# Attention scores and row maxima as pairs of 64-row TensorE tiles, in steps of two PSUM banks

## The reference, cut to what matters

```python
xn = _layernorm(x)
x = x + _L0_attn_ref(xn, Wq, Wk, Wv, Wo) + _L0_ffn_ref(xn, W1, b1, W2, b2)          # full softmax, gelu, 2048 hidden
xn = _layernorm(x)
x = x + _L1_attn_ref(xn, w_qkv, b_qkv, w_dense, b_dense) + _L1_ffn_ref(xn, w12, b12, w3, b3)  # causal, rotary, gate, 512 hidden
# in both attentions: 32 query heads and 8 key heads of 16
scores = jnp.einsum('bhqd,bhkd->bhqk', q, k) * scale
probs = jax.nn.softmax(scores, axis=-1)
out = jnp.einsum('bhqk,bhkd->bhqd', probs, v)
```

## Time and profile before

| | us |
|---|---|
| median of 3 runs | 635.09 (633.90 to 636.69) |
| the profiled execution | 634.52 |
| its span, first to last instruction | 632.8 |
| TensorE matmuls busy in the span | 586.8 (93%) |
| VectorE, ScalarE, GpSimd busy | 438.4, 356.3, 213.8 |
| granted TensorE clock, mean | 0.985 |

### The profile page before, as it was taken

The page is one execution under the profiler, slowest core; times in us unless marked ns, Lnnn a source line. Parts: engine busy times, 40 slices in busy tenths (PEclk is TensorE's granted clock), DMA queues, the critical chain, the costliest instruction groups (busy, mean ns, idle before and its releaser), DMA issues.

```text
span 632.8 us, 10359 instructions
## 1 busy us (share of the span) xinstructions
PE 586.8 (93%) x3360; PEld 452.0 (71%) x3360; DVE 438.4 (69%) x815; ACT 356.3 (56%) x611; POOL 213.8 (34%) x332
## 2 busy tenths in 40 slices
PE   3788899999999999999999999897999999899985
PEld 2677677787777787677877767666777877667754
DVE  6559967656566576486897685867796887487552
ACT  2337766754564683666585564655655564474440
POOL 5703423122303331111322122443643455254231
PEclk9989999999999999999999999999899999999989
DMA  5574541353233334324543323244433353344001
GB/s 187 173 207 151 134 118 67 102 150 101 69 82 103 99 101 118 84 67 134 151 134 100 85 68 117 84 105 114 127 92 102 84 142 110 85 121 116 2 17 51
DMA packets 29805, 67.30 MB, mean 106 GB/s; under 512 B 4788, under 2 KB 17588, under 8 KB 27704
## 3 DMA queue, kind: packets, MB, share of 16 engines
q1 hardware_dynamic: 21112, 38.32, 22.2%
q0 software_dynamic: 8640, 28.32, 15.2%
HBM read 51.67 MB, written 14.68 MB: 105 GB/s over the span
## 4 chain that ended last, share of the span: by engine, by line
PE 74%; ACT 6%; DVE 6%; DMA 5%; issue 5%; POOL 2%; SPq 1%; ACTq 0%; DVEq 0%; POOLq 0%
PE banks L693 48%; PE banks L748 8%; PE banks L800 7%; PE banks L778 7%; PE banks L753 2%; DMA q_sb<-q_parts 2%; DMA raw<-in_attn 1%; PE banks L781 1%; PE banks L713 1%; ACT L917 1%; ACT probs L917 1%; ACT hid_f L937 1%; ACT L936 1%; POOL probs L649 1%; DMA q_sb<-max_t 1%
## 5 line engine op out<-in xcount | busy, mean ns | idle before, releaser
L1067 DVE TENSOR_REDUCE neg_max<-banks 128x2 f32<-128x512 f32 (+1 forms) x256 | 158.1, 620 | 150.4 <-PE banks L748 93.7
L917 ACT ACTIVATE probs<-banks 128x512 f32<-128x512 f32 (+1 forms) x256 | 137.8, 545 | 193.8 <-PE banks L778 145.6
L693 PE MATMUL banks<-xnT,w_up 128*128 128x512 f32 x576 | 157.4, 407 | 5.4 <-issue 3.7
L693 PE MATMUL banks<-w_down,hid 128*128 128x512 f32 x480 | 129.4, 403 | 4.2 <-ACT hid_f L937 2.0
L693 PEld LDWEIGHTS banks<-xnT,w_up 128*128 128x128 f32 x576 | 102.9, 192 | 33.4 <-issue 13.9
L748 PEld LDWEIGHTS banks<-k_sb,q_sb 96*128 96x128 f32 x512 | 93.6, 193 | 22.7 <-issue 5.6
L693 PEld LDWEIGHTS banks<-w_down,hid 128*128 128x128 f32 x480 | 87.0, 191 | 31.8 <-DVE neg_max L1067 6.7
L748 PE MATMUL banks<-k_sb,q_sb 96*128 96x256 f32 (+1 forms) x512 | 100.3, 278 | 4.8 <-DMA q_sb<-q_parts 4.2
L649 POOL TENSOR_SCALAR_AFFINE_SELECT probs<-probs 128x256 f32<-128x256 f32 x128 | 57.6, 450 | 111.5 <-ACT probs L917 106.6
L778 PE MATMUL banks<-q_sb,k_sb 97*128 97x512 f32 x192 | 79.3, 413 | 11.7 <-ACT probs L917 11.1
L693 PE MATMUL banks<-xnT,w_qkv 128*128 128x256 f32 x576 | 83.7, 293 | 2.3 <-DVE xnT L1011 1.4
(11 more groups left out here) (78 smaller groups left out, 629.3 us busy)
## 6 DMA issues: line engine op xcount, KB each, us to landing
q_sb<-q_parts SPq DMA_DIRECT2D x64, 256.0 KB, 4.7
raw<-in_up POOLq DMA_DIRECT2D x48, 256.0 KB, 3.0
raw<-in_down POOLq DMA_DIRECT2D x40, 256.0 KB, 3.0
q_parts<-stage SPq DMA_DIRECT2D x32, 256.0 KB, 2.6
raw<-in_attn POOLq DMA_DIRECT2D x20, 256.0 KB, 3.1
k_parts<-stage SPq DMA_DIRECT2D x16, 256.0 KB, 2.5
k_sb<-k_parts SPq DMA_DIRECT2D x16, 256.0 KB, 4.2
x_res<-in_x SPq DMA_DIRECT2D x4, 512.0 KB, 4.1
```

The costliest lines, as they stand in the source:

```text
L693: mm = nc.tensor.matmul(out_ap, lhs(a), rhs(b_), start=first and j == 0, stop=stop and j == 2, **kw)
L917: nc.scalar.activation(probs[:, i, 0:w], banks[:, ST_BANKS[k % 2], 0:w], ACT.Exp, scale=SCALES[n // B]).then_inc(exp_done, 1)
L1067: nc.vector.tensor_reduce(neg_max[:, s, 2 * g:2 * g + 2, t], banks[:, bank_of[x], :].rearrange("p (r t) -> p r t", r=2)[:, :, 0:w], AX.X, ...
```

## The change

Queries and keys of a head are held as 48 rows (three of 16: the three products of parts), and the maximum is row 48. Half of the heads lie in rows 0 to 48 and the other half in rows 64 to 112, so that a step issues its matmuls in pairs, one in each half of the array's rows, each into a bank of its own. A unit has four steps of `st` and four of `m`, each with four heads and two banks, in slots 0, 2, 4 and 6; an `st` step waits for the exponential of the step before it. `m` has banks 2 and 3 to itself, and three banks are left to the rest. The mask is put in first, by a part of its own ahead of `st`. `pv` stands directly behind `m` in slots 0 and 4, `mt` in slot 4; a down's addition comes behind the next step of TensorE. Keys of two sequences fit. The zeros are gone; the ones come by DMA. GpSimd's clearing is a step of its own (`tri`), one slot behind `st`.

```diff
-ROWS = 96
-MROW = 96
+HALF = 64
+ROWS = 48
+MROW = 48
+SOON = -1
+STEPS = 4
...
 ST_BANKS = (0, 1)
-WORK_BANKS = (2, 3, 4, 5, 7)
+MAX_BANKS = (2, 3)
+WORK_BANKS = (4, 5, 7)
 PV_BANK = 6
 HID = 4
 HT = 4
 
-COST = {"up": 681, "down": 681, "wo": 693, "qkv": 363, "xn": 440, "v": 220, "st": 233, "m": 250, "mt": 110, "pv": 995}
+COST = {"up": 681, "down": 681, "wo": 693, "qkv": 363, "xn": 440, "v": 220, "st": 330, "m": 240, "mt": 110, "pv": 995}
...
+    if x[0] == "m":
+        return 1 if x[1] < LU else 2
     return {"up": 4, "down": 2, "wo": 4, "qkv": 8}.get(x[0], 1)
...
 def cost(x):
+    if x[0] == "part" and x[1][0] == "m":
+        return 300
     return COST.get((x[1] if x[0] == "part" else x)[0], 0)
...
     if x[0] == "down":
-        return [(1, ("add",) + x[1:])]
+        return [(SOON, ("add",) + x[1:])]
     if x[0] == "split":
         return [(1, ("low", x))]
+    if x[0] == "st" and x[1] >= LU:
+        return [(1, ("tri",) + x[1:])]
     return []
...
-    o = []
+    soon, o = [], []
     for g, slot in enumerate(slots):
-        head = [k for k, x in enumerate(slot) if x[0] in ("st", "m")]
+        head = [k for k, x in enumerate(slot) if x[0] in ("st", "m", "pv")]
         cut = head[-1] + 1 if head else 0
         for x in slot[:cut] + due[g] + slot[cut:]:
             o.append(x)
+            if cost(x):
+                o += soon
+                soon = []
             for d, y in followers(x):
                 if d == 0:
                     o.append(y)
+                elif d == SOON:
+                    soon.append(y)
                 else:
                     due[g + d].append(y)
...
-    o += [parts(("qkv", 0, 0)) + [("load_k", 0, 0), ("load_k", 0, 1)]]
+    o += [parts(("qkv", 0, 0)) + [("load_k", 0)]]
-    ms = spread([[("m", 0, i)] for i in range(8)], parts(("qkv", 1, 2)), [1] * 8)
+    ms = spread([[("m", 0, j)] for j in range(STEPS)], parts(("qkv", 1, 2)), [1] * STEPS)
     later = parts(("up", 0, 1, 0)) + parts(("qkv", 1, 0)) + [("bias",)]
-    ms += spread([[("m", 1, i)] for i in range(4)], later, [1] * 4)
-    ms[8] += [("mt", 0), ("mrow", 0)]
-    ms[9] += split(0, "up", 2, 3)
-    ms[10] += split(0, "down", 0, 1)
+    ms += spread([[("m", 1, 0)], [("m", 1, 1)], [], []], later, [1] * 4)
+    ms[4] += [("mt", 0), ("mrow", 0)]
+    ms[5] += split(0, "up", 2, 3)
+    ms[6] += split(0, "down", 0, 1)
...
-    slots = [[("st", u, i)] for i in range(8)]
-    for i in range(8):
-        if i < 4 and u + 1 < UNITS:
-            slots[i].append(("m", u + 1, i + 4))
-        if i >= 4 and u + 2 < UNITS:
-            slots[i].append(("m", u + 2, i - 4))
+    slots = [[] for _ in range(8)]
+    for j in range(STEPS):
+        w, i = (u + 1, j + 2) if j < 2 else (u + 2, j - 2)
+        maxima = parts(("m", w, i)) if w < UNITS else []
+        slots[2 * j] += maxima[:-1] + [("st", u, j)] + maxima[-1:]
+    if u > 0:
+        slots[0].append(("pv", u - 1, 1))
+    slots[4].append(("pv", u, 0))
     if s == 2 and n + 1 < 2 * B:
-        slots[0].append(("load_k", n + 1, 0))
-    if s == 0 and n > 0:
-        slots[0].append(("load_k", n, 1))
+        slots[0].append(("load_k", n + 1))
     if 0 < u < UNITS - 2:
         slots[0].append(("load_q", u + 2))
     if u > 0:
-        slots[1].append(("pv", u - 1, 1))
-        slots[2].append(("norm", u - 1, 0))
-        slots[3] += [("norm", u - 1, 1), ("norm", u - 1, 2)]
-        slots[4].append(("norm", u - 1, 3))
-        slots[5].append(("ctx", u - 1))
+        slots[1].append(("norm", u - 1, 0))
+        slots[2] += [("norm", u - 1, 1), ("norm", u - 1, 2)]
+        slots[3].append(("norm", u - 1, 3))
+        slots[4].append(("ctx", u - 1))
     if u + 1 < UNITS:
-        slots[5] += [("mt", u + 1), ("mrow", u + 1)]
-    slots[5].append(("pv", u, 0))
...
+        if x[0] == "m" and x not in bank:
+            bank[x] = ST_BANKS if x[1] == 0 and x[2] % 2 else MAX_BANKS
+            before[x] = user.get(bank[x])
+            user[bank[x]] = x
+        elif (x in wk or x[0] == "up") and x not in bank:
-        if y:
+        if y and y[0] != "m":
...
-    qscr = nc.dram_tensor("q_parts", (2 * B, S, 2 * HD, UH * T), F32, kind="Internal").ap()
-    kscr = nc.dram_tensor("k_parts", (2 * B, 4, HD, NKV * T), F32, kind="Internal").ap()
+    qscr = nc.dram_tensor("q_parts", (2 * B, S, 2, P, T), F32, kind="Internal").ap()
+    kscr = nc.dram_tensor("k_parts", (2 * B, 2, P, T), F32, kind="Internal").ap()
...
-        q_sb = sb("q_sb", [P, RING, UH, T], F32R)
-        k_sb = sb("k_sb", [P, NKV, T], F32R)
+        q_sb = sb("q_sb", [P, RING, UH // 2, T], F32R)
+        k_sb = sb("k_sb", [P, 2, NKV // 2, T], F32R)
...
+                    sp_.wait_ge(made, ONES)
+                    for row in (MROW, HALF + MROW):
+                        sp_.dma_start(k_sb[row:row + 1, :, :, :].rearrange("o a c t -> o (a c t)").bitcast(F32),
+                                      ones[0:2 * NKV // 2 * T // P, :].bitcast(F32)).then_inc(ones_loaded, 16)
...
-                    if pair < 2:
-                        for j in range(2):
-                            dst = qscr[n, 2 * pair + j].rearrange("(h d) (g t) -> (d g) h t", h=2, g=UH)
-                            sp_.dma_start(dst, stage[:, k % 2, :, j, :].bitcast(F32)).then_inc(staged[k % 2], 16)
-                    else:
-                        for j in range(2):
-                            dst = kscr[n].rearrange("(h e) d (g t) -> e (d g) h t", e=2, g=NKV)[j]
-                            sp_.dma_start(dst, stage[:, k % 2, :, 0, :].bitcast(F32)).then_inc(staged[k % 2], 16)
+                    for j in range(2 if pair < 2 else 1):
+                        dst = qscr[n, 2 * pair + j] if pair < 2 else kscr[n]
+                        sp_.dma_start(dst.rearrange("h q t -> q h t"),
+                                      stage[:, k % 2, :, j, :].bitcast(F32)).then_inc(staged[k % 2], 16)
...
-                    for e in range(2):
-                        sp_.dma_start(q_sb[32 * e:32 * e + 32, u % RING, :, :].rearrange("p g t -> p (g t)").bitcast(F32),
-                                      qscr[n, s]).then_inc(q_loaded[u % RING], 16)
+                        sp_.wait_ge(st_filled, st_index(u - RING, STEPS - 1) + 1)
+                    rows = qscr[n, s].rearrange("h (e a d c) t -> a (h e) d (c t)", e=2, a=2, c=4)
+                    for a in range(2):
+                        to = q_sb[HALF * a:HALF * a + ROWS, u % RING, :, :].rearrange("p c t -> p (c t)").bitcast(F32)
+                        sp_.dma_start(to[0:2 * HD], rows[a]).then_inc(q_loaded[u % RING], 16)
+                        sp_.dma_start(to[2 * HD:], rows[a, 0:2]).then_inc(q_loaded[u % RING], 16)
...
-                    _, n, f = x
-                    k = stg[("store", n, 2)]
-                    sp_.wait_ge(staged[k % 2], 32 * (k // 2 + 1))
-                    if n:
-                        sp_.wait_ge(st_filled, st_index(S * (n - 1) + 2 * f + 1, 7) + 1)
-                    g = slice(4 * f * T, (4 * f + 4) * T)
-                    sp_.dma_start(k_sb[0:4 * HD, 4 * f:4 * f + 4, :].rearrange("p g t -> p (g t)").bitcast(F32),
-                                  kscr[n].rearrange("q d x -> (q d) x")[:, g]).then_inc(k_loaded[f], 16)
+                    n = x[1]
+                    wait_stored(sp_, stg[("store", n, 2)])
+                    if n > 1:
+                        sp_.wait_ge(st_filled, st_index(S * (n - 1) - 1, STEPS - 1) + 1)
+                    rows = kscr[n].rearrange("h (e a d c) t -> a (h e) d (c t)", e=2, a=2, c=4)
+                    for a in range(2):
+                        to = k_sb[HALF * a:HALF * a + ROWS, n % 2, :, :].rearrange("p c t -> p (c t)").bitcast(F32)
+                        sp_.dma_start(to[0:HD], rows[a, 0:2]).then_inc(k_loaded[n % 2], 16)
+                        sp_.dma_start(to[HD:], rows[a]).then_inc(k_loaded[n % 2], 16)
...
-                    sp_.dma_start(q_sb[MROW:MROW + 1, u % RING, :, :].rearrange("o h t -> o (h t)").bitcast(F32),
-                                  max_t[:, u % 2, :].bitcast(F32)).then_inc(m_loaded[u % RING], 16)
+                    for a in range(2):
+                        row = HALF * a + MROW
+                        sp_.dma_start(q_sb[row:row + 1, u % RING, :, :].rearrange("o c t -> o (c t)").bitcast(F32),
+                                      max_t[8 * a:8 * a + 8, u % 2, :].bitcast(F32)).then_inc(m_loaded[u % RING], 16)
...
-            nc.gpsimd.memset(k_sb[64:ROWS, :, :].bitcast(F32), 0.0).then_inc(made, 1)
-            pool.wait_ge(made, 3)
-            load(4)
-            load(5)
-            nc.gpsimd.memset(k_sb[MROW:MROW + 1, :, :].bitcast(F32), 1.0).then_inc(made, 1)
-            pool.wait_ge(made, 4)
-            for k in range(RING):
-                load(6 + k)
-                nc.gpsimd.memset(q_sb[64:ROWS, k, :, :].bitcast(F32), 0.0).then_inc(made, 1)
-                pool.wait_ge(made, 5 + k)
+            for k in range(4, EARLY):
+                load(k)
```

(52 more changed lines are left out.)

102 lines of the change are left out of this document (38 added, 64 removed).

## The result

The changed kernel took 671.88 us in the median of 4 runs (668.45 to 673.13), the kernel before 634.50 (632.97 to 636.69): a ratio of 1.0578, with an interval of 1.0526 to 1.0629. Forecast were 612 us and a gain; what came was 37 us of loss.

The account below looks back on a forecast made before the run. PE's own work was taken to set the time. Terms of -17, -9, -6, -2, +10 and +2 summed to -22 us against 634.5, giving 612.5, called 612, with a range of 597 to 630.

Parts of the forecast that it names:

- the paragraph on DMA and SyncE: Query and key transfers: more loads, fewer key stores, nothing on the path, up to 1 us per sequence either way.
- the slower one: Score and maxima pairs: the two 64-row tiles don't run side by side, giving 656 us; chance 0.07.
- signs of being wrong: Maxima step of 0.36 or 0.47 us, layer 0 PE waits under 5 or over 20 us, or clock falling from 1.00.
- rival 1: Maxima's second pair: weight loads not hidden, 0.36 us in place of 0.24, +15 us, giving 627; chance 0.16.
- Layer 0's groups: Layer 0 scores and maxima: a group of four heads takes 0.67 us instead of 0.94, 64 groups, -17 us.
- pv behind the maxima: pv directly after the maxima: one tile-form change of 0.1 us saved, twice a unit, 32 units, -6 us.
- Layer 1: Layer 1 scores, maxima and masks: 3.5 us a unit instead of 4.1, 16 units, -9 us.
- TensorE's terms: TensorE's savings in layer 0's groups, layer 1 and pv: -17, -9 and -6 us.
- Exponentials: PE's 11.1 us of waits for exponentials: no term of their own; half of them bounded the mask term at -5.
- rival 2: Work banks suffice: PE hardly waits for a bank and exponential waits shrink by 3 us, giving 600 us; chance 0.21.
- Banks and the mask: Three work banks instead of five cost +10 us; the mask going in first costs +2 us over layer 1.
- The start: Start of the run: GpSimd's fills of queries and keys go and unit 0's maxima take four steps, -2 us.

Follow-up runs that it names:

- e1: Changed kernel with scratch rows reordered so each query or key load reads 32 or 16 even rows, stores going out in quadrants: 633.83 us, ratio 1.0028.
- e2: Kernel before with a spare row after each eight of the query scratch, giving its loads a slowest dimension of 4, stores in halves: 706.56 us, ratio 1.1137.
- e4: e1 with each score pair issued twice and, in layer 0, each maxima pair twice: 665.77 us, ratio 1.0534.
- e11: e1, in layer 0 only, with one score step doubled around a met wait, and maxima repeated after two score-form matmuls: 649.32 us in one run.
- e5: e1 with the maxima taking any two free neighbouring banks from a shared pool of five: 632.45 us, ratio 1.0009.
- e8: Changed kernel with its own scratch and stores, loads with slowest dimension 8, plus the five-bank pool of e5: 642.39 us, ratio 1.0152.
- e9: e5 with each slot's query loads issued ahead of the stores due in it: 622.9 us, ratio 0.9837.
- e10: e1 with each slot's query loads issued ahead of the stores due in it: 624.22 us, ratio 0.9837.
- e12: Kernel before with only its query loads put ahead of the store in the same slot: 628.72 us, ratio 0.9953.

## Why the prediction was wrong

**The step that failed** is the paragraph on DMA and SyncE. It counted the loads and their bytes, "four DMAs instead of two", saw 384 KB where there had been 512, and put the path at nothing, up to 1 us per sequence. It never asked over what the new source pattern is spread. Regrouping the rows by half made parts of 4 and 2 the outer dimension of loads whose source had been one even run of rows. The maxima then waited 29.3 + 11.1 us for them. e1 prices it at 35 us, e2 at 74 in the other kernel. None of the four rivals had it; the slower one, tiles that don't run side by side, is refuted by e4. Two of the prediction's own signs of being wrong came: the score step takes 0.34 us where 0.23 to 0.24 stood, and the granted clock of layer 0 fell from 1.00 to 0.98. A third came near, the maxima step of 0.34 beside rival 1's 0.36, and it took e4 to tell an edge from a load that isn't hidden. A price of zero on a transfer whose access pattern changes needs a row of that pattern, and there was none.

**Layer 0's groups**, forecast -17. The streams are as forecast (0.23 and 0.22 to 0.23 of added work in e4), the edges aren't: 0.09 + 0.11 had been read from the old kernel's changes of form, and the changed kernel has 0.11 in each of its two steps, 0.11 behind the group and some 0.05 to 0.08 ahead of it. A group is about 0.85 and not 0.67, so 0.09 less than 0.94: -6 over 64 groups.

**pv behind the maxima**, forecast -6. It came out better: pv starts 0.34 after the maxima like any other successor, takes 1.00 (e4: 187.73 to 188.73), and its way out is the group's. Before, it had cost 1.00 + 0.09 + 0.11. That is 0.20 a time, 64 times: -13.

**Layer 1**, forecast -9. A unit is 4.0 us in the changed kernel's order of time where 4.1 stood before: -2. The same edge is what is missing. Together TensorE's terms are -21 where the sum had -32. The 11 us are a term mis-sized, and would alone have left the time at 623.

**Rival 1**, by which a second load on the same rows isn't hidden, is refuted by e4 and e11: four loads and 512 columns more cost 0.22 us. So for 64-row tiles too the trace disagrees with what the Trainium skill says of loads in TensorE: Matmul & The Clock Gate, section Part 3.

**Exponentials** gained more than any text had: the sum had nothing for them (a gain of 5 was only a bound), rival 2 had 3, and their wait falls from 11.1 to 5.5 in e1, so -6.

**Banks and the mask.** The forecast had +10 for work banks and +2 for the mask. In e1 PE waits 4.6 us for `hid_f` and 4.3 for `xnT`, in the kernel before it waited 2.0 and 2.3 for the same: +5. The masks and the first maxima wait 7.5 + 2.4 us for `neg_max`: +8 or so, as bound, since 1.8 us of such waits were there. The sum was about right, its split wasn't: it is mostly the mask that goes in first, in layer 1. What the pool removes of it buys no time, as e5, e8 and e9 against e10 show.

**The start**, forecast -2. PE's first score comes at 54.8 us in the changed kernel, 50.7 in e1, 51.3 in e10, against 48.8 before. The fills that went were never on this path; the loads of the first unit were, and they are late by 11.7, 7.2 and 7.3 us. That is +6, with wide loads +2.

**The sum again**, for e10: TensorE -21, exponentials -6, start +2, banks and mask +13, the early issue -3 (e12): -15 against 634.5, so 619. PE's busy time bears the first term out: it is 564.3 in e10 and 586.8 before, at nearly the same mean clock (0.983 and 0.985). That e10's profiled execution took just 619.7 is in part luck, since the median of its runs is 5 us higher. For e1 the same terms without the early issue give 622, and 633.8 were measured. What the sum leaves out there is the "issue" wait of 4.4 us and the clock: 0.968 against 0.985 over 632 us is, as an estimate, 11 us of full clock. For the changed kernel the 35 us of narrow loads come on top of e1.

So with loads that keep their spread and are issued in time, the idea behind the change is worth about 1.2% (0.9837 against e12's 0.9953), a third of the 3.5% forecast. Not settled is how much of the lower clock of e1 is owed to its waits and how much to chance, and what in TensorE the edge of a group is.

## What to carry to other kernels

When a change regroups the rows of a load, read the new access pattern's outer dimension before anything else: bytes and counts say nothing of how many DMA engines move them. A load that needs nothing of the newest result should stand in its queue ahead of the store that waits for it. And a price for changing TensorE's tile form that was read in one form is not the price in another.

## What the runs showed of the hardware

- While the last query loads of a slowest dimension of 4 and 2 were under way, the DMA share was 0.11 at 46 GB/s; the same bytes as 32 or 16 even rows land in 2.6 us a load. SyncE takes 0.62 to 0.65 us to issue a narrow load (435.14 and 439.90 above) and 0.37 to 0.42 a wide one (119.00 in e5, 296.28 in e1).
- Two matmuls of 49 rows by 512 columns in the two halves of the array take the time of one, 0.23 us, with the weight loads of the next hidden. Going into such a group and out of it costs about 0.4 us in all (0.85 less two streams of 0.23), whether each step is issued once or twice (e4). In e11 a group of four steps has 0.21 us inside it beyond its streams (1.13 less 0.92), much as a group of two has (0.68 less 0.46).
- A met wait in TensorE's queue costs nothing that shows (e11, 0.57 us with and without).
- After a wait of 7.27 us the granted clock was 0.50, and pv took 1.87 us in place of 1.00; the mean clock was 0.951 in the changed kernel, 0.983 in e10.
- A wait for a load can stand in the profile without a name: e1's 4.35 us "issue" wait and e2's 42.4 us are of a line that waits for query loads, and moving the loads ahead took e1's away.
